# The ninth tile's count stores moved back into the count stage of a graph kernel

## The reference, cut to what matters

```python
# attention layer: h = x as (1250, 12 heads, 64)
a1, a2 = (ft * attn_l).sum(-1), (ft * attn_r).sum(-1)      # ft = h @ W_fc.T, per head
e      = leaky_relu(a1[src] + a2[dst], 0.2)
m      = segment_max(e, dst)
ee     = exp(e - m[dst])
agg    = segment_sum(ee / denom[dst] * ft[src], dst)
x      = layernorm(x + relu(h @ W_res.T + agg))
# three relational layers, three edge types
count  = segment_sum(one_hot(edge_type), dst)              # (node, relation)
agg    = segment_sum((h @ w_rel[edge_type])[src] / count[dst, edge_type], dst)
h      = relu(agg + h @ w_root + bias)
out    = layernorm(x + h)
```

## Time and profile before

| | |
|---|---|
| median of 3 runs | 2428.05 us (2420.83 to 2431.07) |
| profiled execution, its own time | 2421.66 us |
| its span, first to last instruction | 2419.8 us |
| PE busy | 2181.1 us, 90% |
| DVE busy | 1225.3 us, 51% |
| ACT busy | 784.7 us, 32% |
| POOL busy | 461.4 us, 19% |
| attention stage, SP's first instruction | 349.10 us |
| relational stage, first instruction shown of SP | 780.65 us |

### The profile page before, as it was taken

One profiled execution on the slowest core, in us unless ns is written; L12 is line 12 of the kernel. 1 busy time (PEld: TensorE's weight loads), 2 busy tenths in 40 slices (PEclk: granted clock), 3 DMA queues, 4 the chain that ended last, 5 costly groups with the idle time before them and its releaser, 6 DMA issues.

```text
span 2419.8 us, 29974 instructions
## 1 busy us (share of the span) xinstructions
PE 2181.1 (90%) x10968; PEld 1835.2 (76%) x10969; DVE 1225.3 (51%) x1875; ACT 784.7 (32%) x1071; POOL 461.4 (19%) x389
## 2 busy tenths in 40 slices
PE   6999853888887599999999999999999899999997
PEld 2555531333333499999999899999999899999997
DVE  7888767999976633322322432322322342343335
ACT  1133334888885321211211421211211321212212
POOL 0000003999998000000000000000000000000000
PEclk8999975999998699999999999999999999999998
DMA  1134423211110433333432423333333423345332
GB/s 50 45 87 105 105 61 94 76 33 33 33 35 16 137 105 103 111 108 92 115 98 86 120 63 104 111 101 91 116 91 92 131 66 116 105 114 140 99 98 76
DMA packets 138214, 215.26 MB, mean 89 GB/s; under 512 B 87760, under 2 KB 87998, under 8 KB 138073
## 3 DMA queue, kind: packets, MB, share of 16 engines
q1 hardware_dynamic: 97187, 141.08, 20.7%
q0 software_dynamic: 40144, 70.00, 10.1%
q10 hardware_dynamic: 767, 2.57, 0.3%
HBM read 182.51 MB, written 30.70 MB: 88 GB/s over the span
## 4 chain that ended last, share of the span: by engine, by line
PE 59%; DMA 4%; DVE 3%; ACT 1%; issue 0%; ACTq 0%; DVEq 0%
PE banks L1193 30%; PE banks L1165 28%; DMA w_raw<-in_L_gnn_w_root_dram 4%; DVE w_lo L1413 1%; ACT w_hi L1295 1%; PE banks L1217 1%; PE banks L1204 0%; DVE norm_stats L1385 0%; DVE res L1381 0%; PE banks L1235 0%; DVE h_lo L1444 0%; ACT accT L1324 0%; DVE tail_stats L1464 0%; DVE back L1462 0%; ACT accT L1286 0%
## 5 line engine op out<-in xcount | busy, mean ns | idle before, releaser
L1165 PE MATMUL banks<-ct_in,h_hi 125*128 125x416 f32 (+1 forms) x1710 | 603.7, 353 | 0.6 <-ACT accT L1286 0.6
L1165 PE MATMUL banks<-ct_in,h_lo 125*128 125x416 f32 (+1 forms) x1710 | 602.5, 352 | 0.0
L1193 PE MATMUL banks<-g_hi,w_hi 128*128 128x416 f32 (+1 forms) x1440 | 516.5, 359 | 22.5 <-DVE g_lo L1435 22.5
L1193 PE MATMUL banks<-g_hi,w_lo 128*128 128x416 f32 (+1 forms) x1440 | 513.8, 357 | 0.0
L1193 PE MATMUL banks<-g_lo,w_hi 128*128 128x416 f32 (+1 forms) x1440 | 511.2, 355 | 0.0
L1413 DVE TENSOR_TENSOR w_lo<-w_raw,w_hi 128x768 fp32r<-128x768 f32 (+1 forms) x228 | 227.9, 1000 | 474.7 <-ACT w_hi L1295 474.7
L1295 ACT CAST w_hi<-w_raw 128x768 fp32r<-128x768 f32 (+1 forms) x228 | 198.0, 868 | 466.0 <-PE banks L1193 353.7
L939 PE MATMUL head_sums<-pw,x 125*65 125x512 f32 x720 | 274.2, 532 | 59.9 <-POOL pw L723 44.1
L1165 PEld LDWEIGHTS banks<-ct_in,h_lo 125*128 125x128 f32 x1710 | 323.1, 189 | 4.1
L1165 PEld LDWEIGHTS banks<-ct_in,h_hi 125*128 125x128 f32 x1710 | 321.7, 188 | 4.3 <-ACT accT L1286 0.8
L1311 ACT CAST g_hi<-gs 128x416 fp32r<-128x416 f32 (+3 forms) x180 | 97.4, 541 | 700.1 <-DVE gs L1423 700.1
(11 more groups left out here) (198 smaller groups left out, 1565.6 us busy)
## 6 DMA issues: line engine op xcount, KB each, us to landing
w_raw<-in_L_gnn_w_rel_dram SPq DMA_DIRECT2D x117, 384.0 KB, 3.1
ct_in<-s_ct POOLq DMA_DIRECT2D x18, 2031.2 KB, 28.2
w_raw<-in_L_gnn_w_rel_dram SPq DMA_DIRECT2D x54, 448.0 KB, 4.5
ct_in<-s_ct POOLq DMA_DIRECT2D x9, 2041.0 KB, 28.7
s_ct<-ct_stage SPq DMA_DIRECT2D x30, 610.4 KB
w_raw<-in_L_gnn_w_root_dram SPq DMA_DIRECT2D x39, 384.0 KB, 3.1
w_raw<-in_L_gnn_w_root_dram SPq DMA_DIRECT2D x18, 448.0 KB, 5.3
low_spread<-s_low SPq DMA_DIRECT2D x11, 610.4 KB
```

The lines of the kernel that those rows point to most:

```text
L1165: ins = nc.tensor.matmul(pb[0:rows, PA, 0:s.w], a, b, start=j == 0, stop=j == len(pairs) - 1)
L1193: ins = nc.tensor.matmul(pb[:, m, 0:s.w], a, b, start=s.first and j == 0, stop=s.last and j == len(parts) - 1)
```

## The change

Where the stores of the last two tiles are issued. Tile 8 is stored in the count stage like the tiles before it: all three relations and the degrees. Tile 9 is left to the attention stage as a whole, as before. In the count stage SP's stream is then: the two `a_rows` DMAs of tile 8, its four stores, and behind them the two `a_rows` DMAs of tile 9. In the attention stage four stores follow x of head 0 in place of seven.

```diff
-            def tile(tt, b, kept=0):
+            def tile(tt, b, last=False):
                 g = tt * 2 + b
                 sp.wait_ge(rows_split, g * 2 + 2)
                 for m in range(2):
                     sp.dma_start(a_rows[m * H:(m + 1) * H, bass.ds(g * T, T)], splitrow[:, m]).then_inc(rows_out, 16)
-                if kept < R:
-                    tile_staged(sp, tt, b)
-                for r in range(R - kept):
+                if last:
+                    return
+                tile_staged(sp, tt, b)
+                for r in range(R):
                     sp.dma_start(dram["ct"][r].rearrange("(s p) (u c d) -> p s u c d", p=T, c=2, d=T)[:, :, bass.ds(tt, 1), b].rearrange(
                         "p s u d -> p s (u d)"), stage[0:T, b, r]).then_inc(stored[b], 16)
-                if not kept:
-                    sp.dma_start(dram["deg"][bass.ds(g, 1), :],
-                                 stage[T:T + 1, b].rearrange("a r s d -> a (r s d)")).then_inc(stored[b], 16)
+                sp.dma_start(dram["deg"][bass.ds(g, 1), :],
+                             stage[T:T + 1, b].rearrange("a r s d -> a (r s d)")).then_inc(stored[b], 16)
...
-            tile(NT // 2 - 1, 0, kept=2)
-            tile(NT // 2 - 1, 1, kept=3)
+            tile(NT // 2 - 1, 0)
+            tile(NT // 2 - 1, 1, last=True)
             sp.wait_ge(rows_out, 32 * NT)
...
             load_x(0)
-            for b, kept in ((0, 2), (1, 3)):
-                g = NT - 2 + b
-                for r in range(R - kept, R):
-                    sp.dma_start(dram["ct"][r].rearrange("(s p) d -> p s d", p=T)[:, :, g * T:(g + 1) * T],
-                                 stage[0:T, b, r]).then_inc(stored[b], 16)
-                sp.dma_start(dram["deg"][g:g + 1, :], stage[T:T + 1, b].rearrange("a r s d -> a (r s d)")).then_inc(stored[b], 16)
+            g = NT - 1
+            for r in range(R):
+                sp.dma_start(dram["ct"][r].rearrange("(s p) d -> p s d", p=T)[:, :, g * T:(g + 1) * T],
+                             stage[0:T, 1, r]).then_inc(stored[1], 16)
+            sp.dma_start(dram["deg"][g:g + 1, :], stage[T:T + 1, 1].rearrange("a r s d -> a (r s d)")).then_inc(stored[1], 16)
```

## The result

The changed kernel takes 2412.2 us (median, 2411.7 to 2413.7) against 2429.3 us for the kernel before on the same chip: a ratio of 0.9937 (95% interval 0.9913 to 0.9962), faster by 0.63%. A second measurement of the same kernel gave 0.9941 (0.9928 to 0.9954), 14.3 us. The forecast was 13.7 us and 2414.

A forecast was written before the change was run, and what follows sets the result against it. The left-over stores were taken to set the start of the attention stage's steady work. Count stage cost 0 and DVE's sixth y moving from 408.39 to 394.7 gave 2428.05 - 13.7 = 2414 us, range 2405 to 2422.

The forecast's parts named there:

- What sets the start of the attention stage: Attention stage: the left-over stores' landing holds ACT's widening and so POOL's first product, 7.33 us behind it.
- Count stage, cost 0: End of count stage: tile 9's short rows land at about 347.0, before the meeting at 348.9; SP's slack shrinks to 1.9 us.
- the first rival: Count stage: tile 8 lands late at 349.0, short rows 1.3 us behind the meeting; gain 12.4 us, 2415.6; chance 0.13.
- Landing 20 us sooner: Attention stage: tile 9's stores are complete at about 378.6 in place of 398.56, 20 us earlier.
- The low row 1.1 us sooner: Attention stage: with the stores gone at 377.4 the low row lands sooner, DVE's first y at 382.6, before 383.72.
- without sharing: Attention stage: if queues did not share DMA engines, the low row would stay at 383.72 and the gain be 12.6 us.
- DVE's pace and not POOL's: Attention stage: DVE's 13.7 us counts, not POOL's lead of 17.9 us; the rival of POOL's pace had chance 0.07.
- The sum: Whole kernel: 13.7 us of gain, all from DVE's sixth y in the attention stage, giving 2414 us.

The follow-up runs named there:

- Four placements: Tile 8 with all stores, two relations and degrees (kernel before), one and degrees, or none left to the attention stage: sixth y at 66.8, 59.3, 51.8, 46.7 us.

## Why the prediction was right, and which term was off

**What sets the start of the attention stage: right.** Four placements move ACT's stops and the sixth y by 7.5 us for each relation until the low row takes over, and the four kernels without slow stores in the stage have no such wait.

**Count stage, cost 0: right, with a thinner cover than counted.** The short rows landed at 345.9, and SP passed the meeting up to 0.9 us behind ACT. Issuing them elsewhere changed nothing. The start of the attention stage varies by over 2 us with either placement (349.10 and 346.77 before; 346.4 to 348.8 in the profiles with tile 8 stored early and slow stores), so the 2.7 us between the two first profiles need not be the change's. By the first rival it would have cost 1.3 us: not seen.

**Landing 20 us sooner: right**, 20.1.

**The low row 1.1 us sooner: wrong, and the one step that failed.** The step is "With the stores gone at 377.4 the row has the engines for itself", and the 4.9 us that it gave the row. The first y came 34.7 us into the stage, 34.6 before. The slowing by sharing is real on both sides. While both travel, the kernel before shows

```profile
377.00:383.00 6.00, 2.20 (x5) 1.00 (x5) 2.75 (x4) 0.54 (x1) 2.25 (x11) 0.50 0.33 124
```

which is 744 thousand bytes, 625 of them nearly all of the row's. So the stores fell from 83 to some 20 GB/s, and the row needed 6.2 us where it needs 4.8 without stores. But the changed kernel gives the row nothing of this back. Its traffic begins at 27.7 in the stage, still on the tail of the stores, and by the quarter microseconds it ends at 34.1, falling off in steps over the last 1.5 us; with x of head 1 out of the way it still lasts 5.75 us. Only where no slow stores are left in the stage is the uncut row through in 4.8 to 5.0 (tile 9's stores out of the way, or cut). Why a row that starts on the tail of the stores gains nothing was not tested. The Trainium skill's sentence that all sequencers' DMAs interleave on the same 16 engines (DMA: Bandwidth & Descriptors, section Issuing engines are not separate DMA queues) agrees with the trace, where both are slower together. The value that I had named for "without sharing", 12.6 us, is what the stage shows, though by another way: sharing is there, and its gain did not arrive.

**DVE's pace and not POOL's: right.** POOL's lead was 16.5 us at its first product (17.9 forecast) and 12.5 from the tenth on.

**The sum.** 13.7 us were forecast; the stage shows 12.5 to 12.9, and the ratios 14.3 to 15.3. That the forecast 2414 lies so near the measured 2412.2 is partly luck, since it holds 1.1 us that the stage did not give. The intervals of the ratios (from 9.2 and 11.2 us up) hold the stage's figure; the kernel before spreads over 16 us, and that is where I look for it. That is argued and not shown.

## What to carry to other kernels

A store left over to the next stage costs its whole transfer if something there waits for the buffer, and each one moved into an idle stretch of the DMA side pays that back, until another chain is the last to arrive; read that chain's own start before counting on the rest. When two streams share the DMA engines, don't book the gain of both for taking one away: here the stores' loss came back and the low row's did not. And before DMAs are rescheduled, look at their DMA share: at 0.38 of the engines the cure was the shape of the transfer, which made the schedule irrelevant.

## What the runs showed of the hardware that was not expected

A transfer over 125 partitions uses a third of the DMA side: 83 GB/s at a share of 0.38 for 500-byte rows, and 127 GB/s at 0.32 for a large-row load. The same stores as 120 + 5 partitions reach 194 GB/s at 0.90. The Trainium skill has the rule (DMA: Bandwidth & Descriptors, section Why a DMA increments its semaphore by 16 and not by 1): a hardware-queue DMA is spread over the largest number of engines up to 16 that divides the slowest dimension of both sides, which is 5 for 125 and 15 for 120. The large-row load agrees, 0.32 of 16 being 5 engines; the stores' 0.38 is 6, which stays open.

The slow stores delay what another sequencer issues behind them. `s_low` (14.6 KB) took 4.9 us to land behind them and 1.4 us without them, and the low row was through 9.5 us behind its issue and 6.0 without them. Cut stores delay it too: with five relations left to the stage, at 170 GB/s and a share of 0.94, `s_low` took 5.7 us (359.74 to 365.45), but the row still came ahead of DVE's maxima.

From the second head's first y to the end of the attention stage fourteen profiles need 354.9 to 362.0 us with the same instructions on the compute engines. PE's granted clock in windows of 20 us dips there, at other places and by other amounts in each execution: to 0.74 in the longest stretch (362.0) and in the changed kernel's first profile (360.4). That one had 0.83 from 440 to 460 and 0.74 from 500 to 520, where the kernel before had 1.00. That the dips cause the spread was not tested.
